# Mean over heads of a sparse attention: 16 diagonal products replaced by a scaling, a strided sum and two transposes

## The reference, cut to what matters

```python
Q = (x_text @ Wq).reshape(Bb, Tt, H, DH)           # H = 4 heads of 32
K = (x_vision @ Wk).reshape(Bb, Gg, H, DH)
scores = einsum('bthd,bghd->bhtg', Q, K) / sqrt(DH)
topv, topi = top_k(scores, 32)
probs = softmax(topv)
attn = zeros_like(scores).at[..., topi].set(probs)
attn_mean = attn.mean(axis=1)                      # over the heads
V = x_vision @ Wv
c_t = einsum('btg,bgd->btd', attn_mean, V) * text_mask[..., None]
x = layernorm(x_text, g_norm_in, b_norm_in)
scale_in, shift_in = split(c_t @ W_film_in + b_film_in, 2)
x = x * (1.0 + mod_gate * scale_in) + mod_gate * shift_in
```

## Time and profile before

| what | us |
|---|---|
| median of three runs | 5210.79 |
| the profiled execution | 5207.8 |
| its span | 5206.1 |
| TensorE busy, share of the span | 89% |
| VectorE, ScalarE, GpSimd busy | 61%, 38%, 35% |

### The profile page before, as it was taken

How to read it: one execution, slowest core, us unless ns; L and a number is a source line. 1 busy time by engine, 2 the same in 40 slices (tenths; PEclk the granted TensorE clock), 3 DMA queues, 4 the chain that set the end, 5 groups by cost and what they waited for, 6 DMA issues and landing times. The chain is left out here.

```text
span 5206.1 us, 91956 instructions
## 1 busy us (share of the span) xinstructions
PE 4632.5 (89%) x32540; PEld 3600.0 (69%) x32540; DVE 3164.5 (61%) x9688; ACT 1989.8 (38%) x4150; POOL 1816.4 (35%) x2248
## 2 busy tenths in 40 slices
PE   7999587779897899889996999999999977999978
PEld 5666355559675788756664888888888744777755
DVE  6888677758454332067773677777777743444344
ACT  4555255555343232144542333333333322222233
POOL 2222144433254332154440233333333312555522
PEclk9999799989898899999998999999999988999989
DMA  4666311126322322222222111101010054222233
GB/s 116 156 151 157 98 41 55 50 66 180 82 53 32 96 68 73 59 69 72 63 62 73 33 30 30 30 30 30 30 32 28 24 181 161 88 90 92 68 97 106
DMA packets 329714, 397.17 MB, mean 76 GB/s; under 512 B 66021, under 2 KB 289995, under 8 KB 318507
## 3 DMA queue, kind: packets, MB, share of 16 engines
q1 hardware_dynamic: 315946, 366.04, 24.7%
q0 software_dynamic: 13312, 25.25, 2.0%
HBM read 297.64 MB, written 93.55 MB: 75 GB/s over the span
## 5 line engine op out<-in xcount | busy, mean ns | idle before, releaser
L2537 PE MATMUL fa_h<-fa_xnT,fa_w 128*128 128x256 f32 x2048 | 485.1, 383 | 0.0
L2549 PE MATMUL fa_y<-fa_w,fa_hT 128*128 128x256 f32 x2048 | 462.5, 379 | 0.0
L2549 PEld LDWEIGHTS fa_y<-fa_w,fa_hT 128*128 128x128 f32 x2048 | 386.8, 190 | 65.0 <-issue 14.8
L2537 PEld LDWEIGHTS fa_h<-fa_xnT,fa_w 128*128 128x128 f32 x2048 | 382.3, 190 | 71.1 <-issue 13.2
L2416 ACT ACTIVATE fa_hT<-fa_h,fa_b 128x256 f32<-128x256 f32 x512 | 214.5, 470 | 544.1 <-PE fa_h L2537 482.1
L425 DVE TENSOR_REDUCE a_mx<-a_score 128x16 f32<-128x1920 f32 x128 | 276.0, 2156 | 78.9 <-PE a_score L609 78.9
L1021 PE MATMUL f_c_ps<-f_hs,f_diag 64*64 64x256 f32 x3072 | 213.8, 431 | 83.3 <-DVE f_hs L880 83.3
L1563 PE MATMUL r_h<-r_xnT,r_rw 128*128 128x256 f32 x1024 | 248.1, 391 | 16.8 <-ACT r_hT L1521 16.1
L2923 ACT ACTIVATE m_hT<-m_h,m_b 128x256 f32<-128x256 f32 x256 | 107.3, 470 | 404.0 <-PE m_h L2960 404.0
L1703 POOL DMA_INDIRECT e_xg<-moe_rows,e_idx x64 | 128.6, 2009 | 308.8 <-issue 254.8
L1918 PE MATMUL e_h<-e_xT,e_w 128*128 128x256 f32 x1024 | 233.9, 382 | 2.5 <-DVE e_xT L1717 2.5
(11 more groups left out here) (453 smaller groups left out, 11081.0 us busy)
## 6 DMA issues: line engine op xcount, KB each, us to landing
a_floor<-a_lowest SPq DMA_DIRECT2D x64, 960.0 KB, 8.6
cv_toep<-kernels SPq DMA_DIRECT2D x16, 2048.0 KB
x<-a_xo SPq DMA_DIRECT2D x96, 256.0 KB, 4.2
f_xb<-x SPq DMA_DIRECT2D x64, 256.0 KB, 2.8
f_xres<-x SPq DMA_DIRECT2D x64, 256.0 KB, 2.9
a_xb<-x SPq DMA_DIRECT2D x64, 256.0 KB, 2.9
e_w<-in_L_ffn_ew SPq DMA_DIRECT2D x16, 1024.0 KB, 7.7
a_cb<-in_ctx SPq DMA_DIRECT2D x96, 90.0 KB, 2.0
```

The source lines that it names most:

```text
L2537: last = pe.matmul(h_ps[j % 2][:, c, :], w1[:, e, k, f:f + P], xnT[it.p][:, k, :], start=k == 0, stop=k == KD - 1)
L2549: last = pe.matmul(bank[:, t * D:(t + 1) * D], hT[e % 2][:, k, t * P:(t + 1) * P], w2[:, e, k, :], start=k == 0, stop=k == KE - 1)
```

## The change

GpSimd no longer builds diagonals. It multiplies `kept` in place by `share` (`scale_heads`, 128 x 480). A new VectorE step `sum_heads` adds the four heads with a strided reduce into `mean` (128 x 120), and TensorE turns each mean with one transpose. `sum_heads(0)` and `(1)` stand on VectorE behind `weigh_gates`, ahead of `add_expert(0)`. ScalarE's next exponentials wait for the sum instead of the product. On TensorE, `mean_heads` moves behind `up(6)`, `attend` behind `up(7)`, and `film_in(0)`, `turn_x` and `film_in(1)` behind `down(2)`; on ScalarE `aT_out` moves behind `relu(6)`.

```diff
--- before.py
+++ after.py
@@ -2000,7 +2000,7 @@
     sc, left, kept = ([st.sb(f"{n}{t}", [P, NH, SK]) for t in two] for n in ("sc", "left", "kept"))
     top = [st.sb(f"top{t}", [P, ROUNDS, NH, 8]) for t in two]
     wsum, share, nmax = ([st.sb(f"{n}{t}", [P, NH]) for t in two] for n in ("wsum", "share", "nmax"))
-    dg = [st.sb(f"dg{t}", [P, NH, P]) for t in two]
+    mean = [st.sb(f"mean{t}", [P, SK]) for t in two]
     film = [st.sb(f"film{t}", [P, 2 * D]) for t in two]
     km = [st.sb(f"km{p}", [P, SK], U8) for p in two]
     tm = [st.sb(f"tm{p}", [P, TL], U8) for p in two]
@@ -2015,7 +2015,7 @@
     small, large, attn, wready, padded = (st.sem(n) for n in ("small", "large", "attn", "wready", "padded"))
     x_in, r_in, stored, c_in, cv_in, m_in, t_in = ([st.sem(f"{n}{p}") for p in two] for n in (
         "x_in", "r_in", "stored", "c_in", "cv_in", "m_in", "t_in"))
-    cT_out = st.sem("cT_out")
+    cT_out, mean_ready = st.sem("cT_out"), st.sem("mean_ready")
     (stats, roots, xn_ready, x_turned, xT_ready, d_done, d_ready, g_done, gate, exp_ready, ln_ready, w_turned, wT_ready, b_done,
      h_done, h_ready, y_done, summed) = (st.sem(n) for n in (
          "stats", "roots", "xn_ready", "x_turned", "xT_ready", "d_done", "d_ready", "g_done", "gate", "exp_ready", "ln_ready",
@@ -2024,9 +2024,9 @@
      km_ready, v_done, v_ready) = (st.sem(n) for n in (
          "stats3", "roots3", "roots4", "xn3_ready", "xl_scaled", "xl_part", "xl_ready", "x3_turned", "xT3_ready", "q_done", "q_ready",
          "k_ready", "kd_ready", "km_ready", "v_done", "v_ready"))
-    (s_done, pick, nmax_ready, kept_exp, weigh, summed_w, dg_ready, a_done, aT_ready, c_done, cT_ready, f_done, film_ready, mixed,
+    (s_done, pick, nmax_ready, kept_exp, weigh, summed_w, scaled, a_done, aT_ready, c_done, cT_ready, f_done, film_ready, mixed,
      xin_ready) = (st.sem(n) for n in (
-         "s_done", "pick", "nmax_ready", "kept_exp", "weigh", "summed_w", "dg_ready", "a_done", "aT_ready", "c_done", "cT_ready", "f_done",
+         "s_done", "pick", "nmax_ready", "kept_exp", "weigh", "summed_w", "scaled", "a_done", "aT_ready", "c_done", "cT_ready", "f_done",
          "film_ready", "mixed", "xin_ready"))
     PRE, MID = 8, 10
     GATE = PRE + 14
@@ -2164,13 +2164,10 @@
                     pool.tensor_scalar(nmax[t][:], top[t][:, 0, :, 0], -1.0, None, ALU.mult).then_inc(nmax_ready, 1)
                 return step
 
-            def diagonals(t):
+            def scale_heads(t):
                 def step(it):
                     pool.wait_ge(weigh, WEIGH * (2 * it.i + t + 1))
-                    if it.reused(1):
-                        pool.wait_ge(a_done, 2 * it.i + t - 1)
-                    pool.tensor_tensor(dg[t][:], const["ident"][:].unsqueeze(1).to_broadcast([P, NH, P]),
-                                       share[t][:].unsqueeze(2).to_broadcast([P, NH, P]), ALU.mult).then_inc(dg_ready, 1)
+                    pool.tensor_tensor(kept[t][:], kept[t][:], share[t][:].unsqueeze(2).to_broadcast([P, NH, SK]), ALU.mult).then_inc(scaled, 1)
                 return step
 
             def mix(t):
@@ -2186,7 +2183,7 @@
                 return step
 
             pipeline(pool, B, DEPTH, [
-                (6, roots_of_sum), (6, roots_of_normed), (6, key_mask), (6, affine), (6, spread_k), (7, diagonals(0)), (7, diagonals(1)),
+                (6, roots_of_sum), (6, roots_of_normed), (6, key_mask), (6, affine), (6, spread_k), (7, scale_heads(0)), (7, scale_heads(1)),
                 (6, negate_max(0)), (6, negate_max(1)), (1, roots_of), (7, mix(0)), (7, mix(1))])
 
         @block.vector
@@ -2354,7 +2351,7 @@
                     if t == 0:
                         dve.wait_ge(t_in[it.p], 16 * (it.h + 1))
                     if it.reused(1):
-                        dve.wait_ge(dg_ready, 2 * it.i + t - 1)
+                        dve.wait_ge(scaled, 2 * it.i + t - 1)
                     c = Chain(dve, weigh, 2 * it.i + t, WEIGH)
                     c.add(dve.tensor_reduce(wsum[t][:], kept[t][:], AX.X, ALU.add))
                     c.add(dve.tensor_scalar(tmf[t][:, 0:1], tm[it.p][:, t:t + 1], 1.0 / NH, None, ALU.mult))
@@ -2364,6 +2361,14 @@
                     c.add(dve.tensor_scalar(share[t][:], wsum[t][:], tmf[t][:, 0:1], None, ALU.mult))
                 return step
 
+            def sum_heads(t):
+                def step(it):
+                    dve.wait_ge(scaled, 2 * it.i + t + 1)
+                    if it.reused(1):
+                        dve.wait_ge(a_done, 2 * it.i + t - 1)
+                    dve.tensor_reduce(mean[t][:], kept[t][:].rearrange("p h k -> p k h"), AX.X, ALU.add).then_inc(mean_ready, 1)
+                return step
+
             def film_out(t):
                 def step(it):
                     dve.wait_ge(f_done, 2 * it.i + t + 1)
@@ -2375,7 +2380,7 @@
 
             pipeline(dve, B, DEPTH, [
                 (6, sum_stats), (7, pick_round(2)), (6, norm_sum), (4, rank_gates), (5, begin_sum), (7, pick_round(3)), (7, keep_taken),
-                (7, weigh_heads(0)), (7, weigh_heads(1)), (4, weigh_gates), (5, add_expert(0)), (6, take_scores), (6, pick_round(0)),
+                (7, weigh_heads(0)), (7, weigh_heads(1)), (4, weigh_gates), (7, sum_heads(0)), (7, sum_heads(1)), (5, add_expert(0)), (6, take_scores), (6, pick_round(0)),
                 (5, add_expert(1)), (4, wT_out), (1, norm_stats), (7, film_out(0)), (6, pick_round(1)), (2, norm), (5, add_expert(2)),
                 (7, film_out(1)), (5, add_expert(3))])
 
@@ -2448,7 +2453,7 @@
                 def step(it):
                     act.wait_ge(nmax_ready, 2 * it.i + t + 1)
                     if it.reused(1):
-                        act.wait_ge(a_done, 2 * it.i + t - 1)
+                        act.wait_ge(mean_ready, 2 * it.i + t - 1)
                     for h in range(NH):
                         last = act.activation(kept[t][:, h, :], sc[t][:, h, :], ACT.Exp, bias=nmax[t][:, h:h + 1])
                     last.then_inc(kept_exp, 1)
@@ -2471,7 +2476,7 @@
 
             pipeline(act, B, DEPTH, [
                 (4, d_out), (5, relu(0)), (5, relu(1)), (5, relu(2)), (5, relu(3)), (6, xT3_out), (6, scale_rows), (4, exps), (5, relu(4)),
-                (6, k_out), (6, q_out), (5, relu(5)), (7, aT_out), (5, relu(6)), (7, cT_copy), (5, relu(7)), (6, head_exps(0)),
+                (6, k_out), (6, q_out), (5, relu(5)), (5, relu(6)), (7, aT_out), (5, relu(7)), (7, cT_copy), (6, head_exps(0)),
                 (6, head_exps(1)), (3, xT_out)])
 
         @block.tensor
@@ -2582,11 +2587,8 @@
                 if it.followed(1):
                     pe.wait_ge(pick, PICK * (it.i + 1) + TL)
                 for t in range(TL):
-                    pe.wait_ge(pick, PICK * (it.i + 1) - TL + t + 1)
-                    pe.wait_ge(dg_ready, 2 * it.i + t + 1)
-                    for h in range(NH):
-                        last = pe.matmul(a_ps[0:SK, t * P:(t + 1) * P], kept[t][:, h, :], dg[t][:, h, :], start=h == 0, stop=h == NH - 1)
-                    last.then_inc(a_done, 1)
+                    pe.wait_ge(mean_ready, 2 * it.i + t + 1)
+                    pe.transpose(a_ps[0:SK, t * P:(t + 1) * P], mean[t][:], const["ident"][:]).then_inc(a_done, 1)
                 pe.wait_ge(cv_in[it.p], 16 * (it.h + 1))
                 for k in range(2):
                     last = pe.matmul(a_ps[0:SK, S:2 * S], cv[it.p][:, k, :], wv[:, k, :], start=k == 0, stop=k == 1)
@@ -2610,8 +2612,8 @@
 
             pipeline(pe, B, DEPTH, [
                 (4, difficulty), (5, up(0)), (4, gates), (5, up(1)), (5, up(2)), (5, bias), (5, up(3)), (6, turn_sum),
-                (5, up(4)), (5, down(0)), (6, project), (5, down(1)), (6, scores), (5, up(5)), (4, turn_weights), (7, mean_heads), (5, up(6)), (7, attend),
-                (5, up(7)), (7, film_in(0)), (3, turn_x), (5, down(2)), (7, film_in(1)), (5, down(3))])
+                (5, up(4)), (5, down(0)), (6, project), (5, down(1)), (6, scores), (5, up(5)), (4, turn_weights), (5, up(6)), (7, mean_heads),
+                (5, up(7)), (7, attend), (5, down(2)), (7, film_in(0)), (3, turn_x), (7, film_in(1)), (5, down(3))])
     st.end()
```

## The result

The changed kernel takes 5168.06 us, median of four runs (5162.31 to 5174.90), against 5212.26 for the kernel before, here the median of four (5209.38 to 5215.35; 5210.79 was that of the first three): a ratio of 0.9916, 95% interval 0.9898 to 0.9933. It is faster, by 44 us; 48 were forecast, and 5168 lies in the range of 5155 to 5182. The profiled execution was the slowest of the four, 5174.9 us with a span of 5173.2.

A forecast was written before the change was run, and what follows sets the result against it. TensorE was taken as the bound, a steady slot costing its instructions' time. Saving 46 us in steady slots and 2 in the tail, 48, takes the profiled 5207.8 to 5160; 3.0 up to the median gives 5163, range 5155 to 5182.

The forecast's parts named there:

- TensorE's saving: Steady slots: two transposes (0.22 us) replace 16 product records (1.75), saving 1.53 us in each of 30 slots, 46 us.
- The reduce: VectorE's strided sum over heads: 0.98 us each, 1.96 a slot, bounds 0.64 and 1.73, hidden in VectorE's slack.
- the 0.11 us for the fixed part: VectorE's new reduce: 0.11 us added to 0.87 us for 480 elements at L888's rate.
- The scaling: GpSimd's in-place multiplication of 480 elements, two a slot: 1.0 us each, bounds 0.99 and 1.2.
- The ring's slack: VectorE-TensorE loop through film product, picks, sums, take_scores and mean: 1.5 us to spare in the steady slot, just not binding.
- the wait of VectorE before film_out(0): VectorE's wait for the first film product in a steady slot: near 5 us, given as a sign of being right.
- ScalarE (c): Rival: ScalarE's copies late for attend under up(7), 0.2 to 1 us a slot, 6 to 30 us lost, 5169 to 5193; 5%.
- the clock in the steady part (d): Rival: transposes leave TensorE at half clock for 1.75 us a steady slot, 7 us slower, 5216 with the tail; 2%.
- nothing gained (e): Rival: modelled ends of matmuls hide another bound, the steady slot stays 42.02 us, time 5211; 2%.
- The tail: Last items, where TensorE waits: -2 us, bounds -5 and +3; low clock on attend and film products might cost up to 4.3.
- the 2.5 us counted for it: Tail, item 30: gain near 2.5 us from the shorter mean, the scaling being mostly past.

The follow-up runs named there:

- e2: Changed kernel with TensorE and ScalarE put back in the old order, new scaling, sums and transposes kept: 5167.82 us, ratio 0.9915 to the kernel before.
- e5: Changed kernel with each strided reduce made three times, extra results unread: 5219.67 us in one timed execution, beside 5202.65 for the kernel before on that visit.
- e9: The changed kernel again, unaltered, on another chip: 5116.69 us against 5157.81 for the kernel before on that visit, ratio 0.9918.
- e3: Changed kernel with GpSimd's affine moved behind the two scale_heads: 5172.81 us in one time, stage 1337.4 us against the changed kernel's 1345.3.
- e6: Changed kernel with unread products on TensorE, 28 ahead of the last turn_sum and 9 ahead of the last mean: 5165.44 us, ratio 0.9923 to the kernel before.
- e1: Kernel before with only the new TensorE and ScalarE orders, diagonals and product records kept: 5212.05 us against 5212.54, ratio 0.9998.
- e4: Changed kernel with each strided reduce made twice, first result unread: stage 1362.5 us against the changed kernel's 1345.3; no whole time given.

## Why the prediction was right, and where it was off

**TensorE's saving (1.53 us a slot, 46 us): right.** The transposes cost 0.22, the slot 40.49 to the hundredth. From the first values' product to the end of the last down(3) it went from 1231.2 to 1186.9, 44.2 less; 29 x 1.53 and the 1.73 of an up(6) that moved out of this stretch would be 46.1. Of the missing 1.9, 1.75 are the five long slots (0.33 + 0.38 + 0.37 + 0.34 + 0.33). The prediction checked the ring with durations from one undisturbed slot; it did not ask which instructions of VectorE and GpSimd stand side by side there with 0.1 us between their starts, though keep_taken and affine did (0.11 us, e2 and the kernel before), with the later film products moving one of the two to 0.03; and it did not ask what the waits that it reported gone had been good for. That is the step that failed, small as it was.

**The reduce (0.98 us): right**, 977 ns. That is 2.04 ns an element, near the 1.80 of L888, and 8.1 ns an output, far from its 14.4. The 0.11 us for the fixed part was an estimate; reduces of 4 elements take 149 and 152 ns in the kernel before (L379, L378). The new reduce is dearer than the contiguous one of 643 ns; why, no run shows. **The scaling (1.0): right**, 986 ns.

**The ring's slack (1.5 us): a size off.** It is 2.2 to 2.3, and the wait of VectorE before film_out(0) 5.69 and not 5.0. Half of the 0.8 is that two reduces in a row take 1.8 us from start to start and not 2.0, and that take_scores lost the 0.2 between its two halves; the rest is spread over ends that overlap the next start and a VectorE that is 0.1 us late and not 0.2. The mechanism, the wait for take_scores, was the right one; e5 shows it.

**ScalarE (c), the clock in the steady part (d), nothing gained (e): did not happen.** attend follows up(7) without a wait, and the slot is shorter. The granted clock is 1.00 from 2930 to 4110 us with ten transposes a slot before and with twelve after.

**The start: 0.6 us missed.** It grew by 0.8 where the order accounts for 1.73 - 1.53 = 0.2; the first up(0) ran longer at the low level, 3.57 us instead of 2.99, with 0.52 granted over it instead of 0.62.

**The tail (-2): not gained, inside its bounds** of -5 and +3, at +1.5 in the first profile and +0.1 in e9. The prediction named the cause as a risk, up to 4.3 us for attend and film products at the lower level, and took too little of it. Measured from the last values' product to the end: 10.8 us before, 14.6 after (13.1 in e9), so 3.8 lost (2.4), where the shorter last mean saved 2.2. Nor did item 30 give the 2.5 us counted for it: from the last turn_sum to the last mean it is 38.1 us before and 37.6 after, because its own attend and film products took 2.05, 3.78 and 2.80 us instead of 1.10, 3.43 and 2.18.

The terms measured: -44.2 + 0.8 + 1.5 = -41.9 for the stage, where -48 stood. The medians say -44, with an interval that holds both. That the time came within 5 us of the forecast rests on the steady part, which was right for the reason given; that the misses of the tail, the start and the long slots stayed small against it is no merit of the prediction.

## What to carry to other kernels

Where one engine is busy without a gap at full clock, its instruction time is the forecast, and a sum over the records removed and added can hold to the hundredth of a microsecond (here 40.49 us forecast and measured, with 199.88 of 200 us busy at 1.00); spend the remaining care on which pairs of instructions on other engines start within a tenth of each other (here 0.03 us). A reordering that only gives an engine more room can still cost, if it takes away the waits that soak up small delays and keep two contending instructions in a fixed order; here it cost 1.8 us of 5168, too little to see in the time, and both repairs (the old order, or the contender moved away) were a few words in the lists of steps. In a drain phase, work removed from TensorE may be paid back by the clock of what follows (here 2.4 to 3.8 us), and two profiles of one kernel can differ there by as much as the change is worth.

## What the runs showed of the hardware

- GpSimd's affine and VectorE's keep_taken hold each other up where they overlap, and the one that starts first keeps its time, ahead by as little as 0.03 us: in the changed kernel affine takes 2.3 us instead of 1.27 behind keep_taken (2.24 in the kernel before, 0.11 us behind it), keep_taken 3.1 to 3.3 us instead of 1.22 behind affine. The strided tensor_reduce was never held: 958 to 1004 ns over all 64 in the changed kernel.
- What makes VectorE 0.2 to 0.35 us late in just the 2nd, 8th, 11th, 17th and 26th slot is a pause of 0.09 to 0.27 us between two instructions of VectorE, which the profile gives to nothing. It stands before the same instructions in all seven profiles with the same VectorE list (changed, e2, e3, e6 to e9), on two chips; in the 17th slot of the changed kernel:

```profile
3606.30 1.58 DVE L2331 MAX8 fa_top<-fa_left 128x8 f32<-128x120 f32 x8 [0.27 <-issue]
```

  In the 17th slot of e2, where the waits for down(3) and the bias swallow it and keep_taken starts on time:

```profile
3605.79 1.58 DVE L2331 MAX8 fa_top<-fa_left 128x8 f32<-128x120 f32 x8 [0.27 <-issue]
```

  The kernel before has such pauses too, in its 4th, 6th, 18th, 25th and 27th slot, the 18th:

```profile
3662.95 1.58 DVE L2334 MAX8 fa_top<-fa_left 128x8 f32<-128x120 f32 x8 [0.27 <-issue]
```

  It swallows them in the same way; e1, with its VectorE list and the new order, has its collisions in just these five slots and in the 2nd. Two more pauses of the changed kernel, in its 23rd and 28th slot, don't delay keep_taken. Counted in VectorE's records of the trace, waits for semaphores included, its seven pauses lie 1153, 639, 1152, 1280, 512 and 384 records apart, and those of the kernel before 384, 2305, 1407 and 384: multiples of 128 to within one, as in e4 and e5. So in these runs the pauses go with the place in VectorE's list, and not with what other engines do. What makes them, no run shows; and most multiples of 128 show no pause.
- The kernel before took 5212, 5213, 5203 and 5158 us as a median on four visits, the last two on one chip. The stage of the change started at 2842.06 in one profile of the changed kernel and at 2785.95 in the other, but lasted 1345.3 and 1344.1: the difference lies in earlier stages. Comparisons across visits would have drowned the 44 us: e9's 5117 beside the first visit's 5212 would have doubled them.
